# A mixture-of-experts decoder block: combine weights spread by DMA and multiplied in by GpSimd

## What is computed

```
scores = softmax(xf @ gate_w.T)          # 16 experts; the 2 best of the 2 best groups of 4 are kept
combine = (one_hot(idx, E) * weights[..., None]).sum(1)
h1 = einsum('td,edi->tei', xf, We1) + be1
h3 = einsum('td,edi->tei', xf, We3) + be3
h = silu(h1) * h3
yo = einsum('tei,eid->ted', h, We2) + be2
y = einsum('te,ted->td', combine, yo)
z = silu(xf @ ws1 + bs1) * (xf @ ws3 + bs3) @ ws2 + bs2
return y + z
```

## Time and profile before

| what | us |
|---|---|
| median of 3 runs | 1150.1 |
| the runs | 1147.67, 1150.1, 1152.42 |
| span of the profiled execution (its only time) | 1150.6 |
| busy PE, DVE, ACT, POOL | 975.8, 788.8, 577.3, 227.7 |

### The profile page before, as it was taken

The page is one execution under the profiler, slowest core; times in us unless marked ns, Lnnn a source line. Parts: engine busy times, 40 slices in busy tenths (PEclk is TensorE's granted clock), DMA queues, the critical chain, the costliest instruction groups (busy, mean ns, idle before and its releaser), DMA issues.

```text
span 1150.6 us, 22137 instructions
## 1 busy us (share of the span) xinstructions
PE 975.8 (85%) x9069; PEld 767.2 (67%) x9069; DVE 788.8 (69%) x1841; ACT 577.3 (50%) x1148; POOL 227.7 (20%) x220
## 2 busy tenths in 40 slices
PE   6656899969998799978999699987999689987687
PEld 5553688737785587846886487855787477864566
DVE  3256866687866967678667878678666867669444
ACT  4434755367534665357553565346652575445322
POOL 6001410035000520024100440014200341004100
PEclk9886999979998899979999799989999799997789
DMA  5300010000100010000100010000100000000000
GB/s 146 80 1 1 2 38 1 11 10 2 38 10 10 2 38 1 11 10 2 37 11 1 11 31 8 10 11 2 38 1 10 11 2 1 10 11 1 1 1 19
DMA packets 28902, 18.36 MB, mean 16 GB/s; under 512 B 7649, under 2 KB 27394, under 8 KB 28802
## 3 DMA queue, kind: packets, MB, share of 16 engines
q1 hardware_dynamic: 26914, 12.48, 4.2%
q0 software_dynamic: 1280, 4.20, 1.2%
q10 hardware_dynamic: 608, 0.27, 0.1%
HBM read 12.62 MB, written 4.19 MB: 15 GB/s over the span
## 4 chain that ended last, share of the span: by engine, by line
PE 62%; DVE 21%; ACT 10%; POOL 3%; issue 3%; SPq 1%; DMA 0%; DVEq 0%; POOLq 0%
PE banks L510 7%; PE banks L674 5%; PE banks L491 5%; PE banks L493 5%; PE banks L492 5%; PE banks L606 4%; PE banks L624 4%; ACT M L867 3%; PE banks L648 3%; DVE PXUT L1222 3%; DVE mx L1221 3%; PE banks L769 3%; PE banks L541 2%; DVE sil L1166 2%; PE banks L598 2%
## 5 line engine op out<-in xcount | busy, mean ns | idle before, releaser
L874 ACT ACTIVATE sil<-banks,b 128x512 f32<-128x512 f32 x144 | 99.5, 691 | 199.6 <-PE banks L493 197.2
L867 ACT COPY M<-banks 128x512 f32<-128x512 f32 x208 | 122.9, 609 | 90.3 <-PE banks L624 70.2
L1166 DVE SCALAR_TENSOR_TENSOR sil<-banks,b,sil 128x512 f32<-128x512 f32 x128 | 95.8, 749 | 93.6 <-ACT sil L874 91.8
L510 PEld LDWEIGHTS banks<-w,hT 128*128 128x128 f32 x1152 | 151.5, 194 | 12.5 <-issue 7.2
L510 PE MATMUL banks<-w,hT 128*128 128x128 f32 x1152 | 154.5, 277 | 1.4 <-DVE hT L1173 1.4
L389 POOL DMA_DIRECT2D out_x<-xn x16 | 12.9, 809 | 534.3 <-DVE xn L1179 534.3
L426 POOL TENSOR_TENSOR PXUT<-PXUT,rx 128x512 f32<-128x512 f32 x80 | 87.2, 1117 | 101.7 <-DVE rx L1235 101.7
L1173 DVE TENSOR_TENSOR hT<-sil,banks 128x512 f32<-128x512 f32 x128 | 87.9, 687 | 25.1 <-PE banks L500 21.3
L624 PE MATMUL banks<-ident,PXUT 128*128 128x128 f32 x384 | 61.9, 301 | 31.7 <-ACT M L867 28.2
L598 PE MATMUL banks<-maskb,pick 32*64 32x512 bf16 x512 | 46.4, 506 | 46.6 <-ACT PXUT L930 28.2
L674 PEld LDWEIGHTS banks<-pooled,A 128*128 128x128 f32 x512 | 66.1, 207 | 19.9 <-DVE pooled L1286 18.6
(11 more groups left out here) (199 smaller groups left out, 2067.2 us busy)
## 6 DMA issues: line engine op xcount, KB each, us to landing
xin<-in_x SPq DMA_DIRECT2D x8, 512.0 KB, 4.1
cin<-in_ctx SPq DMA_DIRECT2D x8, 512.0 KB, 5.3
out_x<-xn POOLq DMA_DIRECT2D x16, 256.0 KB, 2.8
KQ<-in_L_attn_Wqkv SPq DMA_DIRECT2D x3, 512.0 KB, 5.3
KQ<-in_L_ffn_We SPq DMA_DIRECT2D x2, 512.0 KB, 4.6
KQ<-in_L_attn_Wo SPq DMA_DIRECT2D x1, 512.0 KB, 8.0
w<-in_L_ffn_We SPq DMA_DIRECT2D x1, 512.0 KB
woM<-xwT SPq DMA_DIRECT2D x16, 8.0 KB, 1.8
```

Of the source, the lines that this page charges most:

```text
L510: mm(ps(name)[:, P * t:P * t + P], hT[:, k % 2, P * t:P * t + P], w2[:, pair[k], :], start=(n == 0 and t == 0), stop=False, skip_group_che ...
L867: cp(dst, ps(name)[:] if src is None else src).then_inc(ready, 1)
L874: nc.scalar.activation(sil[:, k % 2, :], ps(f"H1_{k}")[:], ACT.Silu, bias=b1[:, pair[k]:pair[k] + 1]).then_inc(sil_ready, 1)
L1166: V.scalar_tensor_tensor(sil[:, k % 2, :], ps(f"H3_{k}")[:], b3[:, p:p + 1], sil[:, k % 2, :], ALU.add, ALU.mult).then_inc(hid_ready, 1)
```

## The change

Every combine weight row is spread by DMA: combT, now transposed right after the gate, is stored to a DRAM tensor (comb_d), and for each routed unit SP loads the rows of its two experts to 64 partitions each, into cw of four slots. GpSimd multiplies sil by it in place. DVE's hidden is then one operation for every unit. combs, combsT, spread, onehot3, identb and the matmuls of weight are gone; the bank of C becomes the second one of H3; gate goes to the bank of Y and the transposes of comb to that of H1. The down product follows two units behind up, with sil and hT of three slots. xnT3 shares the memory of e1, so that DVE's soften waits for lo_ready. result(e, 0) stands after hidden(e, 10).

```diff
@@ -41,6 +41,7 @@
     CHUNKS = TOK // CH
+    LAG, CW = 2, 4
     EPS = 1e-5
@@ -64,11 +65,9 @@
     RINGS = {"att": (att, 4),
-             "h1": (["xnT3_0"] + [f"H1_{k}" for k in range(UNITS)], 1),
-             "h3": (["xnT3_1"] + [f"H3_{k}" for k in range(UNITS)], 1),
-             "c": (["gate", "combS"] + [f"C_{k}" for k in PAIRED if k < EP + 1] + ["combT_0", "combT_1"]
-                   + [f"C_{k}" for k in PAIRED if k > EP], 1),
-             "y": (["Y_0", "Y_1"], 1),
+             "h1": (["xnT3_0", "H1_0", "H1_1", "combT_0", "combT_1"] + [f"H1_{k}" for k in range(2, UNITS)], 1),
+             "h3": (["xnT3_1"] + [f"H3_{k}" for k in range(UNITS)], 2),
+             "y": (["gate", "Y_0", "Y_1"], 1),
@@ -188,16 +184,16 @@
-        combs = sb("combs", [P, T, P], bf16)
         combT = sb("combT", [P, TOK])
-        combsT = sb("combsT", [P, TOK], bf16)
-        sil = sb("sil", [P, 2, CH])
-        hT = sb("hT", [P, 2, CH])
+        sil = sb("sil", [P, LAG + 1, CH])
+        hT = sb("hT", [P, LAG + 1, CH])
+        cw = sb("cw", [P, CW, CH])
+        comb_d = nc.dram_tensor("comb_d", [E, TOK], fp32)
...
         banks = [two[k // 2][:, 512 * (k % 2):512 * (k % 2) + 512] for k in range(8)]
-        bank = {"att": banks[0:4], "h1": banks[4:5], "h3": banks[5:6], "c": banks[6:7], "y": banks[7:8],
+        bank = {"att": banks[0:4], "h1": banks[4:5], "h3": banks[5:7], "y": banks[7:8],
@@ -328,11 +320,31 @@
                 sp.dma_start(w_sb[:, E:E + 2, :], ws.rearrange("d (e i) -> d e i", i=EI)).then_inc(loaded_e, 16)
+            def weights_spread(e):
+                sp.wait_ge(combT_ready, 2 * e + 2)
+                sp.dma_start(comb_d.ap(), combT[0:E, :]).then_inc(comb_stored, 16)
+                sp.wait_ge(comb_stored, 16 * e + 16)
+                for n, k in enumerate(PAIRED):
+                    use = len(PAIRED) * e + n
+                    c, p = k // (EP + 1), pair[k]
+                    if use >= CW:
+                        sp.wait_ge(weighted, use - CW + 1)
+                    for a in range(2):
+                        row = comb_d.ap()[2 * p + a, CH * c:CH * c + CH]
+                        sp.dma_start(cw[EI * a:EI * a + EI, use % CW, :],
+                                     row.partition_broadcast(EI)).then_inc(cw_loaded[use % CW], 16)
             for g in range(1, GROUPS):
...
                 sp.dma_start(cin[:], c_v[g]).then_inc(c_loaded, 16)
+                if g >= 2:
+                    weights_spread(g - 2)
+            for e in (GROUPS - 2, GROUPS - 1):
+                weights_spread(e)
@@ -355,20 +366,13 @@
                                          pattern=[[-1, P]], channel_multiplier=1))
-            nc.gpsimd.tensor_copy(identb[:], ident[:]).then_inc(consts, 1)
-            nc.gpsimd.memset(woM[:], 0.0)
+            nc.gpsimd.memset(woM[:], 0.0).then_inc(consts, 1)
             nc.gpsimd.memset(Vb[:], 0.0)
             nc.gpsimd.memset(xnT[:, TOK:TOK + S], 0.0)
-            nc.gpsimd.memset(combs[:], 0.0)
             nc.gpsimd.memset(combT[:], 0.0)
@@ -381,8 +385,17 @@
                                                  base=32 * a, pattern=[[-1, S]], channel_multiplier=1))
-            nc.gpsimd.tensor_copy(spread[:].rearrange("r p a i -> r (p a) i"),
-                                  onehot3[:].unsqueeze(2).to_broadcast([P, E, EI])).then_inc(consts, 1)
+            nc.gpsimd.memset(comb[:, :, E:E + 1], 1.0).then_inc(consts, 1)
+            def weight(e, k):
+                if e is None or k not in PAIRED:
+                    return
+                use = len(PAIRED) * e + PAIRED.index(k)
+                pool.wait_ge(cw_loaded[use % CW], 32 * (use // CW) + 32)
+                pool.wait_ge(sil_ready, UNITS * e + k + 1)
+                s = sil[:, k % (LAG + 1), :]
+                nc.gpsimd.tensor_tensor(s, s, cw[:, use % CW, :], ALU.mult).then_inc(weighted, 1)
             def store(e, c):
@@ -409,11 +422,15 @@
                                             ALU.add).then_inc(xr_ready, 1)
+                for k in range(EP + 4):
+                    weight(e, k)
                 if e is not None:
...
                     nc.gpsimd.tensor_tensor(rstda[:], va[:], mhalf[:], ALU.pow).then_inc(rstd_ready, 1)
+                for k in range(EP + 4, UNITS):
+                    weight(e, k)
                 if e is not None:
@@ -492,14 +509,6 @@
-            def weight(e, k):
-                name = f"C_{k}"
-                c = k // (EP + 1)
-                wait_free(pe, e, name)
-                mm(ps(name)[:], spread[:, pair[k], :, :], combsT[:, CH * c:CH * c + CH], start=True,
-                   stop=True).then_inc(fulled(name), 1)
             def down_to(e, k):
@@ -507,10 +516,10 @@
                 for t in range(4):
-                    mm(ps(name)[:, P * t:P * t + P], hT[:, k % 2, P * t:P * t + P], w2[:, pair[k], :],
+                    mm(ps(name)[:, P * t:P * t + P], hT[:, k % (LAG + 1), P * t:P * t + P], w2[:, pair[k], :],
                        start=(n == 0 and t == 0), stop=False, skip_group_check=True)
                 if n == EP:
-                    pe.wait_ge(combT_ready, 3 * e + 2 + c)
+                    pe.wait_ge(combT_ready, 2 * e + 1 + c)
                     for t in range(4):
@@ -521,14 +530,8 @@
                 up(e, k)
-                if k in PAIRED:
-                    weight(e, k)
-                if k == EP + 1:
-                    turn_comb(e, 0)
-                if k:
-                    down_to(e, k - 1)
-                if k == EP + 1:
-                    turn_comb(e, 1)
+                if k >= LAG:
+                    down_to(e, k - LAG)
             def scores_1(g, n):
@@ -734,22 +737,14 @@
                 if e is not None:
-                    down_to(e, 0)
-                    up(e, 2)
-                    wait_free(pe, e, "combS")
                     pe.wait_ge(comb_ready, e + 1)
-                    for t in range(T):
-                        last = turn_over(ps("combS")[:].bitcast(bf16)[:, P * t:P * t + P], combs[:, t, :], identb[:])
-                    last.then_inc(fulled("combS"), 1)
-                    pe.wait_ge(combT_ready, 3 * e + 1)
-                    weight(e, 1)
+                    turn_comb(e, 0)
+                    turn_comb(e, 1)
+                unit(e, 2)
                 if g is not None:
...
                     scores_2(g, 1)
-                if e is not None:
-                    down_to(e, 1)
-                    weight(e, 2)
                 unit(e, 3)
@@ -812,7 +807,8 @@
                 if e is not None:
-                    down_to(e, 17)
+                    for k in range(UNITS - LAG, UNITS):
+                        down_to(e, k)
                 if g is not None:
@@ -871,7 +867,7 @@
                 wait_full(act, e, f"H1_{k}")
-                nc.scalar.activation(sil[:, k % 2, :], ps(f"H1_{k}")[:], ACT.Silu,
+                nc.scalar.activation(sil[:, k % (LAG + 1), :], ps(f"H1_{k}")[:], ACT.Silu,
                                      bias=b1[:, pair[k]:pair[k] + 1]).then_inc(sil_ready, 1)
             def probs_moved(g, q):
@@ -980,7 +976,9 @@
                 if e is not None:
-                    moved(e, "combS", combsT[:], combT_ready, ps("combS")[:].bitcast(bf16))
+                    for n in range(2):
+                        moved(e, f"combT_{n}", combT[0:2 * E, 512 * n:512 * n + 512], combT_ready,
+                              ps(f"combT_{n}")[0:2 * E, :])
                 for k in range(2, 5):
@@ -1006,10 +1004,6 @@
                 silu(e, 9)
-                if e is not None:
-                    for n in range(2):
-                        moved(e, f"combT_{n}", combT[0:2 * E, 512 * n:512 * n + 512], combT_ready,
-                              ps(f"combT_{n}")[0:2 * E, :])
                 for k in range(10, 16):
@@ -1132,45 +1126,23 @@
                     link_e(V.tensor_tensor(oh[:, k], oh[:, k], g2[:].unsqueeze(2).to_broadcast(te), ALU.is_equal))
                     if k == 0:
                         link_e(V.scalar_tensor_tensor(tv[:], oh[:, 0], -FARTHER, tv[:], ALU.mult, ALU.add))
-                        hidden_3(e, 1)
                 link_e(V.tensor_tensor(tv[:], oh[:, 0], oh[:, 1], ALU.add))
-                cw = comb[:, :, 0:E]
-                part = [combs[:, :, E * k:E * k + E] for k in range(3)]
-                V.tensor_tensor(cw, tv[:], orig[:], ALU.mult)
-                link_e(V.tensor_tensor(part[0], tv[:], orig[:], ALU.mult))
-                V.tensor_tensor(ga[:], cw, part[0], ALU.subtract)
-                link_e(V.tensor_tensor(part[1], cw, part[0], ALU.subtract))
-                V.tensor_tensor(part[2], ga[:], part[1], ALU.subtract).then_inc(comb_ready, 1)
+                V.tensor_tensor(comb[:, :, 0:E], tv[:], orig[:], ALU.mult).then_inc(comb_ready, 1)
             def hidden(e, k):
-                if k not in PAIRED:
-                    wait_full(dve, e, f"H3_{k}")
+                wait_full(dve, e, f"H3_{k}")
+                if k in PAIRED:
```

(29 more changed lines are left out.)

28 lines of the change are left out of this document (8 added, 20 removed).

## The result

The changed kernel takes 1160.3 us, median of seven runs (1154.7 to 1164.2), against 1150.1 (1145.2 to 1153.3, seven runs) for the kernel before: a ratio of 1.0095, 95% interval 1.0066 to 1.0125. It is **slower by about 1%**. The profiled execution spans 1161.1 us (1150.6 before), at a mean granted clock of 0.911 (0.921 before).

A forecast was written before the change was run, and what follows sets the result against it. In the expert stage PE is seldom idle while DVE and ACT wait for it. From 1150.6, +7.7 for seven middle repetitions (+1.1 each), -1.5 last repetition, -3.0 set-up: 1154 us; range 1136 to 1172, the forecast's own 1147 to 1161.

The forecast's parts named there:

- Set-up -3.0: Set-up: with constants, selects and a copy removed, everything behind GpSimd's constants moves 3.0 us earlier.
- The new wait on PE: Start of the expert stage: PE idle some 4.0 of 4.6 us for ACT's comb copies, queued behind the key copies.
- Store and first load 5.1: Start of the expert stage: storing the combine weights and landing the first load take 5.1 us, ends 4.2 and 7.5.
- Second transposes 2.1 late, 0.8 more for the clock: Transposes of the second probabilities come 2.1 us late; lowered TensorE clock behind the wait adds 0.8 at hidden 3.
- Units 6 to 10, -2.0: Units 6 to 10: five spreading matmuls fewer (-1.1 us), two comb transposes already paid (-0.9).
- Units 11 to 15, +0.4 and 0.7 for the clock: Next xn transposes 0.4 us late, weight 12 queued behind GpSimd's power; half of a 1.5 us clock cost counted as 0.7.
- Units 16 and 17, -0.85: Units 16 and 17: two spreading matmuls fewer, -0.45 us; DVE's first maximum 4.2 after the unit's start instead of 4.6.
- Softmax stage 0: Stage behind the first maximum is DVE's and stays unchanged; the extra down product falls where PE waits for ACT.
- Last repetition -1.5: Last repetition: spreading matmuls (-3.1 us) and transposes (-0.9) saved, less DMA, GpSimd and clock costs, giving -1.5.
- quick loads: Rival: weight loads land in 1.8 us and the clock is kept; -1.2 a repetition, 1137 us, chance 0.26.
- slow loads: Rival: store and first load take 7.5 us, hidden 1 onward 2.4 later, eight times; 1173 us, chance 0.20.
- GpSimd holding DVE off: Rival: GpSimd's multiplications stall DVE's normalisations and apply through the shared port, 0.65 us each; 1163 us, chance 0.12.

The follow-up runs named there:

- experiment 3: Changed kernel without the store and loads of the combine weights, GpSimd multiplying by a constant 0.5: 1160.2 us in one run, span 1156.8.
- experiment 4: Changed kernel with PE kept busy by 20 identity transposes behind the first comb transpose and 6 behind the second: 1156.9 us in one run.
- experiment 2: Changed kernel with ACT's comb copies ahead of the key copies: 1147.3 us, ratio 0.9975 to the kernel before.
- experiment 6: Changed kernel with down product 16 ahead of the scores and only 17 behind them: 1172.6 us in one run.
- experiment 1: Changed kernel with weight 12 ahead of the norm's power on GpSimd: 1169.9 us, ratio 1.0192 to the kernel before.
- experiment 5: On top of experiment 2, DVE instead of GpSimd multiplies the weights of units 12 to 14: 1128.4 us, ratio 0.9801 to the kernel before.
- experiment 8: As experiment 5, but DVE multiplies all sixteen weights of a repetition, GpSimd none: 1120.3 us in one run.
- experiment 7: On top of experiment 2, the second comb transpose in a bank of its own (ring of Y): 1147.0 us, ratio 0.9954 to the kernel before.

## Why the prediction was right, and where it was not

Forecast 1154, measured 1160.3: inside the range of 1136 to 1172, and just inside the forecast's own, 1147 to 1161. The forecast itself stood at +0.3%, which by its own words can hardly be told from none; it added 3.2 us to the span, and 10.5 were measured. To "slower" the prediction gave its two slow rivals (0.20 and 0.12) and a part of the forecast's 0.40. The steps:

- **Set-up -3.0:** measured -3.2. Right, and for the reason given.
- **Gate 1.7 earlier:** 1.5. Right.
- **The new wait on PE:** right in place and cause. The forecast let PE begin the first comb transpose at 561.2 and the second copy end at 566.1, 4.9 later; they stand at 563.19 and 567.92, 4.7. PE was idle 3.1 of it (2.47 and 0.66), not 4.0: the second transposes took 1.04 instead of 0.61, at the halved clock.
- **Store and first load 5.1:** 5.3, from 567.95 to 573.26. Right. The page's row for the load says 2.9, where I had 2.35, and the store took 1.9 to the issue of the first load, where I had 2.1. The Trainium skill's figures ("DMA: Bandwidth & Descriptors", anatomy of one DMA), given there for a transfer that GpSimd issues, make an estimate of 5.1 in the same sum, and not the 5.0 that I wrote. Both were close, and the trace decides for 5.3. It hardly mattered: experiment 3 shows that without any load at most 4 us of 1161 go away, with the gate in the way there.
- **Second transposes 2.1 late, 0.8 more for the clock:** measured 3.55. The clock's term was the one mis-sized: experiment 4 puts it at 1.4. I had let silu 3 come 1.5 later, hidden by the weights; it came late enough to decide hidden 3 itself (577.38). I named the wait, and its cause in ACT's queue, but not how cheap it was to remove: experiment 2.
- **Units 6 to 10, -2.0:** -1.8 at full clock, in five repetitions; in the two others the clock halved within them and they took 25.1. The mean is -1.4.
- **Units 11 to 15, +0.4 and 0.7 for the clock:** +1.9; in the two repetitions at full clock it is +1.4, so the clock's part is 0.5. The three terms that I added up there, -1.1, -0.9 and 2.7, make 0.7 and not 0.4. The wait of 2.7 at unit 14 was 2.52. What I left out of the sum is the apply beside the weights: its half took 2.29 instead of 1.10. I had this as a rival, with 0.65 us an operation read from one gate row, chance 0.12. It is real, larger per place, and in one place of the repetition only. Forecast and rival were not exclusive; the time lies between them.
- **Units 16 and 17, -0.85:** -0.46. The spreads went; the extra 0.4 before the maximum did not come.
- **Softmax stage 0:** measured -1.5. **This step failed.** I had written that one down product more stands after the scores "where PE waits for ACT anyhow", at no cost. It had a gain: with it the second group of scores keeps the full clock, and DVE waits 0.99 us for it instead of 1.6 to 2.0, which experiment 6 takes away again. That is some 0.8 of the 1.5; another 0.6 come from the second wait shown there, whose cause is open.
- **Last repetition -1.5:** the seventh and the last together gave +0.2; with the seventh's share of +2.1 that leaves about -1.9. Right in sign and size.

So the sum was +1.1 and became +2.1 a repetition, seven times. The errors partly cancelled: +0.65 and +0.6 and +0.8 and +0.4 missed, -1.5 missed the other way. That the time lies inside the forecast's own range is in part luck: with the softmax stage at 0, as forecast, the other misses would have made about 1171.

The rivals: quick loads (1137) fell with the 5.3 us, and so did slow loads (1173). The border that I gave for these, 5.8 us, was itself mis-worked: by my own eight times the difference, the whole is over 0.5% slower from 5.4 us on, just above what was measured. GpSimd holding DVE off (1163) is real; experiments 1, 5 and 8 show it. It has its place in the 0.8 us by which units 11 to 15 missed, of 2.45 that were missed in all that way. What remains open is why the half clock appears in some repetitions of one execution and not in others: units 6 to 10 are 23.5 to 23.8 or 25.1, the softmax stage 44.5 or 45.3 to 45.6, with the same instructions.

What the change got wrong is thus settled. Two choices cost the gain: the comb copies' place in ACT's queue (experiment 2, 13 us) and GpSimd as the engine that multiplies (experiments 5 and 8, 27 us), which DVE did not need to be relieved of. With both put right the rest of the change, which takes the weights off PE and adds the lag and the second bank, is worth 25 to 31 us. No run takes the weights off PE without the lag and the bank, so these shares are not told apart, except in units 6 to 10, where PE's work that is gone or has moved (2.0 by the forecast) accounts for the 1.8.

## What to carry to other kernels

Before work is moved to an idle engine, look at what it will run beside: the multiplication had got a slower engine, a place behind a 1.66 us power and a neighbour that it stalls, while DVE had the room at 0.69. When a copy is added to a queue, put it by who waits for it, not by where its data arrive. And a piece of work placed into a wait of PE can be worth more than its own time, because of the clock behind the wait; two short waits joined into one can cost as much as they saved (experiment 7).

## What the runs showed of the hardware

- **GpSimd's multiplication holds off DVE's tensor_scalar from SBUF to SBUF, for its whole length.** Mean of the 64 operations of the apply: 343 ns before, 495 in the changed kernel, 661 in experiment 1, 342 in experiments 5 and 8. Of the four that took 4.08 us in experiment 1, the three that start beside a multiplication take 1.29, 1.32 and 1.37 us and end 0.1 behind it; the one between two multiplications takes 0.34. GpSimd's own stays at 1.25 to 1.28. A gate operation on DVE with two inputs in SBUF takes 1.24 instead of 0.29 in the same way (experiment 3). DVE's scalar_tensor_tensor, which reads PSUM and one SBUF tile, takes 0.75 us wherever it runs beside a multiplication (at 619.78 above), as before without one: not held off. The Trainium skill, "SBUF — State Buffer", section on SBUF's two sides, says that an operation in a two-port mode takes the pair of ports as an exclusive lock, and the other waits. The prediction said that no run showed this kind against GpSimd. These traces agree with it for tensor_scalar, though they do not name the mode.
- **It goes the other way too.** GpSimd's power on 8 columns, beside DVE's product of two SBUF tiles in experiments 5 and 8:

```profile
L434 POOL TENSOR_TENSOR norm_a<-norm_a,mhalf 128x8 f32<-128x8 f32 x8 | 16.6, 2074 | 94.9 <-DVE norm_a L1069 94.9
L410 POOL TENSOR_TENSOR norm_a<-norm_a,mhalf 128x8 f32<-128x8 f32 x8 | 13.3, 1662 | 22.1 <-DVE norm_a L1069 22.1
```

  The eight that run in the expert stage take 0.41 us longer than the eight of the same form elsewhere.
- **TensorE's clock** fell to 0.50 behind the wait of 2.5 us at 564 (in all seven repetitions, also where it came as 0.95 and 1.4) and behind that of 2.5 at 618 (in five of seven). It stayed at 1.00 through waits of 0.27 and 0.92 around 638 with the extra down product ahead of them, and fell where 0.63, 0.46 and 0.93 followed each other (before, and experiment 6). The price was 1.4 us at the first place (experiment 4), 0.5 on the mean at the second, and 0.8 to 1.3 in the softmax stage (experiment 6).
- **A row of DRAM spread to 64 partitions,** 128 KB written, took 2.9 us to land (median of 256, 2.6 to 4.7); the load of 512 KB, four times as large, took 4.1. GpSimd waited for a load 14 times out of 128, always with one of the first three weights of a repetition.
